# A state-space layer and an expert layer in one kernel: carried state folded into the products, first y products on ScalarE, expert weights split one step earlier

## The chip, the cores and the metric

The kernel runs on one core of one Trainium2 chip. Its metric is the device time of one execution in microseconds; the median of three runs before the change is 4197.73 us (4197.45 to 4197.76). Engines are named as in the profile: PE (TensorE), DVE (VectorE), ACT (ScalarE), POOL (GpSimd), SP (SyncE).

## The reference, cut to what matters

The input x is 8 images of 384 channels and 1024 tokens (32 x 32). Layer 0 adds to x a selective state-space block of the group-normed input; layer 1 adds a mixture of four experts of the group-normed result.

```
x = x + L0(group_norm(x))                 # 32 groups of 12 channels
  t  = layernorm(t);  xm, z = split(t @ in_proj.T)          # 384 -> 2 x 768
  xc = silu(causal_conv3(xm) + conv_b)                      # 3 taps along the tokens
  dt, B, C = split(xc @ x_proj.T)                           # 24, 16, 16
  dt = softplus(dt @ dt_proj.T + dt_b)
  h[l] = exp(dt[l] * A) * h[l-1] + (dt[l] * xc[l]) * B[l]   # 768 channels x 16 states
  y = sum_n h[l, :, n] * C[l, n] + D * xc;  y = y * silu(z)
  t = gelu(y @ out_proj.T @ w1.T + b1) @ w2.T + b2
x = x + L1(group_norm(x))
  scores = softmax(x @ gate_w + gate_b);  the two best experts weigh w
  out = sum_e coef_e * (relu(x @ w1_e + b1_e) @ w2_e + b2_e)
```

All of it is in float32. In layer 1 every operand is split into a high and a low part in fp32r, and three products of these take the place of one.

## The kernel before, in words

**Layer 0** works on 16 units, each half an image (512 tokens; the first half of an image has `half` 0, the second `half` 1). It runs as a software pipeline of 18 steps, n = -1 to 16: in step n unit n is scanned ("mid"), unit n + 1 is prepared ("pre": layer norm MU and VAR, projection and convolution XM, XP, C's transposition CT, dt DT), and unit n - 1 is finished ("post": y's transposition Y, output projection O, MLP M1 and M2). Step -1 is the prologue: it has no scan.

The scan of a unit has 32 slots k, 16 states in each of two groups of 384 channels; a slot has three scans of 128 channels x 512 tokens. In a slot POOL forms the product `vv` = (dt * xc) * B for all three (`scan_pool`, L575), two buffers deep; ACT forms exp(dt * A) into one of two PSUM banks (`scan_act`, L586); DVE scans them into `hh` (`scan_dve`, L615). PE transposes `hh` 128 tokens at a time (`scan_pe`, L675) into one of two banks `ht`, and DVE multiplies each of these four pieces by C and adds it to y (`mac_dve`, L661; for state 0 it is a plain product, L659). One of the four pieces in some states ("spread", by SPREAD_MASK) goes to ACT and POOL instead (L633, L645). A scan of a second half starts from the last column of the first half's scan, which ACT copied to `hl` (`last_act`, L593).

What lies between the scans is set by a written-out ORDER of stages for PE, with pads, and by LAGS, which say how many slots after PE's work the stage's ACT, DVE and POOL parts stand in their engines' own order. Each engine executes its instructions in that order. DVE takes up to DVE_QUOTA dense instructions after a scan. SP issues nearly all loads; POOL issues those of the gate and of the expert weights.

**The prologue.** DVE computes the group statistics of the first image (`group_stats`), then its own part of the preparation of unit 0; between them it computes `bn_stats` of the 14 other half images (`stat_dve`, L1172), all queued behind its first instruction of that step. The products over groups (L321) multiply by a 384 x 384 matrix `group`, nine blocks. At the end of the prologue the aggregates of the other images go through the same chain (`rest_dve`, `rest_act`, `rest_pe`), DVE, PE, DVE, PE, ACT, DVE, ahead of the first scan. For unit 0, POOL forms the layer norm's product with rstd (L920), the convolution's sums (L967) and the two products with dt (L1060, L1062).

**The last step** (n = 16) has no scan. PE runs O, M1, M2 of the last unit and, between them, the gate's logits of seven images, for which POOL loads x1 back (`gate_load`, L1218). After these loads POOL loads the raw expert weights w1, w2 (2.36 MB each, L1509) into `big`.

**Layer 1** begins with the gate of the last image: statistics (L233, L321 to L332, L340), logits (L275), top 2. Meanwhile ACT rounds the raw weights to `we_hi` (`split_act`, L1856) and POOL subtracts (`split_pool`, L1849) to `we_lo`, four of each at the start and four after. The first unit's products with w1 (`first_mm`) are spread in PE's order between the gate's. Then a loop over the units follows, bound by PE.

Of the kernel before, what the change touches and what calls it, by code (L numbers as in the profile page):

```python
# [13 lines left out]

# [11 lines left out]
P = 128  # L26
# [21 lines left out]
DVE_QUOTA = 1  # L48

# [4 lines left out]
ORDER = ("Y3 Y4 Y5 pad:3:0:3 DT3 pad:5:0:10 DT4 GN0 pad:5:19:6 O0 O1 DT5 O2 MU0 M1.0 pad:1:0:0 "  # L54
# [4 lines left out]
LAGS = {"Y.dve": 1, "Y.pool": 1, "Z.act": 0, "O.act": 0, "M1.act": 0, "M2.dve": 1, "MU.dve": 1,  # L59
        "MU.act": 2, "VAR.act": 0, "VAR.pool": 5, "XM.act": 0, "XM.pool": 2, "XM.act2": 2,  # L60
        "XP.act": 7, "XP.sync": 1, "CT.dve": 8, "DT.act": 1, "DT.pool": 5, "GN.act": 3,
# [14 lines left out]

DENSE_SLOTS = 31
SPREAD_LAG = 3
# [6 lines left out]
BURST_QUOTA = 3  # L85
SPREAD_MASK = 10818
# [6 lines left out]
MACS = [(k, c) for k in range(SLOTS) for c in range(CH) if not spread(k, c)]  # L93
# [42 lines left out]
def build(nc, a, out):  # L136

    with ExitStack() as ctx:
# [8 lines left out]
        w_d = nc.dram_tensor("top_weights", (KTOP, NB, L), F32).ap()  # L147

# [16 lines left out]
        layer0(nc, a, sem, psum, ident, st1, gn0, eps, x_d, x1_d, b_d, big, vv, consts, gate)  # L165
        layer1(nc, a, sem, psum, ident, eps, x1_d, w_d, out_d, consts, big, gate)
# [136 lines left out]

def group_stats(dve, act, pe, dv, ac, pc, mv, group, bank, tmp, gn, eps, tag, affine=False,
# [9 lines left out]
    if pe is not None:  # L314
        for src, dst, mark in ((mv[:, :, :, 0], mean_ps, "mean"), (tmp, var_ps, "var")):
# [3 lines left out]
            for m in range(KC):  # L319
                for k in range(KC):  # L320
                    mm = pe.matmul(dst[:, m, :], group[:, k, m * P:(m + 1) * P], src[:, k, :],  # L321
                                   start=(k == 0), stop=(k == KC - 1))
# [29 lines left out]
def layer0(nc, a, sem, psum, ident, st1, gn0, eps, x_d, x1_d, b_d, big, vv, consts, gate):  # L352
    with ExitStack() as ctx:
# [35 lines left out]
        hl = sb("hl", [P, NS, KD])  # L389
        yy = sb("yy", [P, CH, DI])  # L390
# [88 lines left out]
        e_da, e_v, e_scan = ev("dA", SLOTS * G3), ev("v", SLOTS), ev("scanned", SLOTS * G3)  # L479
        e_ht, e_mac, s_hl = ev("hT", SLOTS * CH), ev("mac", len(MACS)), sem("h_last")  # L480
        e_sc, e_ad = ev("scaled", len(SPREADS)), ev("added", len(ADDS))
# [51 lines left out]

        def bank_free(eng, units, name, i):


            pos = place[(name, i)]
            same = [s for q, s in enumerate(order[:pos]) if q % NDB == pos % NDB and s[0] in units]
# [30 lines left out]
        def scan_pool(eng, u, k):  # L569
            g, n = scan_of(k)  # L570
            if n == 0:
# [3 lines left out]
            e_v.inc_by(eng.tensor_tensor(  # L575
                vv[:, k % 2, :, :], wu[:, G3 * g:G3 * g + G3, :],
                bb[:, k % NBB:k % NBB + 1, :].to_broadcast([P, G3, T]), ALU.mult))
# [22 lines left out]
        def scan_dve(eng, u, k, i):  # L600
            g, n = scan_of(k)
            j = G3 * g + i
            if i == 0:
# [7 lines left out]
                elif k >= 2:  # L611
                    wait_last(eng, u, k - 2)
# [908 lines left out]
def layer1(nc, a, sem, psum, ident, eps, x1_d, w_d, out_d, consts, big, gate):  # L1521
    with ExitStack() as ctx:
# [345 lines left out]
        def first_mm(eng, q):  # L1868

            u, e, m = Unit(0, 0), q // KC, q % KC  # L1870
            if m == 0:
                eng.wait_ge(s_wlo, e + 1)
# [160 lines left out]
```

## Time and profile before

| | us |
|---|---|
| median of 3 runs | 4197.73 |
| the profiled execution, its own time | 4199.85 |
| its span, first to last instruction | 4198.2 |
| first scan | 93.44 |
| last step of layer 0 ends, layer 1 begins | about 3372 |
| PE, DVE, ACT, POOL busy | 3836.2, 3485.8, 2588.7, 2585.2 |

The times in the profile are microseconds from the span's start. "Busy" adds up recorded durations; where an engine starts an instruction before the record of the one before has ended, these overlap, so that time in a row is read from the starts. "Idle before" an instruction names the event that ended the idle time. PE's float32 matmul of 512 columns is two instructions in the trace.

### The profile page before, as it was taken

What the parts mean: (1) busy time and instruction counts of PE and PEld (TensorE: products, weight loads), DVE (VectorE), ACT (ScalarE), POOL (GpSimd) and SP (SyncE); (2) the same over time, 40 slices, a digit from 0 to 9 for tenths busy, and PEclk for the clock granted to TensorE, in tenths of its full rate; (3) what the DMA queues carried; (4) which work ended last, traced back from release to release, by engine and by line L of the source; (5) the groups of instructions that cost most, each with busy time, mean ns of one, the idle gap of its engine ahead of it and who ended that gap; (6) DMA issues with size and microseconds to landing.
All of it is one profiled execution on the core that took longest, in us unless ns stands there. A gap on an engine that the chain in (4) does not pass through costs nothing. (4 is left out here: it accounts for less than half of the span.)

```text
span 4198.2 us, 48613 instructions
## 1 busy us (share of the span) xinstructions
PE 3836.2 (91%) x15575; PEld 2300.2 (55%) x15575; DVE 3485.8 (83%) x4627; ACT 2588.7 (62%) x4102; POOL 2585.2 (62%) x1314
## 2 busy tenths in 40 slices
PE   6679898989998989989898989899979979999999
PEld 4344545455444544544544455445544468888887
DVE  5899999999999999999999999999999155555555
ACT  4667676767677776767676767676755233343433
POOL 3778787777878787878787878778876120000000
PEclk8779999999999999999999999999989989999999
DMA  5122222222222222222222222222222511111110
GB/s 179 43 70 66 89 67 85 73 83 78 84 68 88 69 89 88 70 92 66 88 66 89 67 85 80 82 72 88 64 83 74 202 56 53 40 40 40 40 40 36
DMA packets 147748, 317.90 MB, mean 76 GB/s; under 512 B 15388, under 2 KB 15772, under 8 KB 147012
## 3 DMA queue, kind: packets, MB, share of 16 engines
q1 hardware_dynamic: 139936, 281.74, 20.7%
q0 software_dynamic: 6832, 28.99, 1.9%
q10 hardware_dynamic: 756, 4.44, 0.3%
q8 instruction: 109, 1.79, 0.2%
q14 instruction: 115, 0.94, 0.1%
HBM read 289.36 MB, written 25.76 MB: 75 GB/s over the span
## 5 line engine op out<-in xcount | busy, mean ns | idle before, releaser
L575 POOL TENSOR_TENSOR vv<-big,bb 128x1536 f32<-128x1536 f32 x512 | 1767.4, 3453 | 595.1 <-DVE hh L615 579.8
L586 ACT ACTIVATE bank<-big,a_neg 128x512 f32<-128x512 f32 x1536 | 1045.3, 689 | 795.4 <-DVE hh L615 791.2
L675 PEld LDWEIGHTS bank<-ident,hh 128*128 128x128 f32 x6144 | 758.6, 146 | 1092.1 <-DVE yy L661 508.1
L675 PE MATMUL bank<-ident,hh 128*128 128x128 f32 x6144 | 1026.6, 289 | 258.0 <-DVE yy L661 161.9
L661 DVE SCALAR_TENSOR_TENSOR yy<-bank,ct,yy 128x384 f32<-128x384 f32 x1760 | 1036.1, 601 | 135.5 <-PE bank L675 131.8
L615 DVE TENSOR_TENSOR_SCAN hh<-bank,hl,vv 128x512 f32<-128x512 f32 x768 | 972.2, 1273 | 25.5 <-ACT bank L586 14.5
L615 DVE TENSOR_TENSOR_SCAN hh<-bank,vv 128x512 f32<-128x512 f32 x768 | 926.3, 1214 | 37.5 <-POOL vv L575 19.1
L795 PE MATMUL bank<-tt,wring 128*128 128x512 f32 x1152 | 556.4, 596 | 17.1 <-ACT tt L781 16.3
L826 PE MATMUL bank<-hid,wring 128*128 128x512 f32 x1152 | 553.0, 596 | 1.8 <-DVE xr L842 1.8
L1745 POOL DMA_DIRECT2D out<-xb x16 | 12.2, 765 | 777.3 <-DVE xb L1740 777.3
L1696 ACT ACTIVATE big<-bank,vv 128x512 f32<-128x512 f32 x180 | 123.9, 688 | 366.7 <-PE bank L1601 366.7
L932 PE MATMUL bank<-xn,w_in 128*128 128x512 f32 x576 | 285.0, 607 | 7.2 <-POOL xn L920 5.0
L747 PE MATMUL bank<-xn,w_in 128*128 128x512 f32 x576 | 283.6, 598 | 0.0
L771 PE MATMUL bank<-xc,w_out 128*128 128x512 f32 x576 | 278.5, 600 | 0.0
L1715 DVE TENSOR_TENSOR big<-big 128x512 f32<-128x512 f32 x188 | 126.9, 689 | 176.6 <-ACT big L1696 176.6
L795 PEld LDWEIGHTS bank<-tt,wring 128*128 128x128 f32 x1152 | 192.2, 191 | 135.0 <-issue 108.3
L826 PEld LDWEIGHTS bank<-hid,wring 128*128 128x128 f32 x1152 | 194.8, 192 | 124.1 <-issue 120.9
L967 POOL TENSOR_TENSOR xc<-xc,xm 128x510 f32<-128x510 f32 x192 | 226.1, 1179 | 23.0 <-ACT xc L957 15.4
L1599 PE MATMUL bank<-hb_hi,we_hi 128*128 128x512 f32 x576 | 225.7, 392 | 6.3 <-DVE hb_lo L1720 6.3
L1599 PE MATMUL bank<-xg_hi,we_hi 128*128 128x512 f32 x576 | 225.5, 391 | 0.0
L1600 PE MATMUL bank<-hb_lo,we_hi 128*128 128x512 f32 x576 | 225.4, 391 | 0.0
L1601 PE MATMUL bank<-hb_hi,we_lo 128*128 128x512 f32 x576 | 225.4, 391 | 0.0
(179 smaller groups left out, 5027.1 us busy)
## 6 DMA issues: line engine op xcount, KB each, us to landing
bb<-b_rows SPq DMA_DIRECT2D x512, 256.0 KB, 3.3
wring<-in_w_m SPq DMA_DIRECT2D x192, 384.0 KB, 3.1
xn<-in_x SPq DMA_DIRECT2D x16, 768.0 KB, 4.7
xr<-in_x SPq DMA_DIRECT2D x16, 768.0 KB, 6.1
x_scratch<-xr SPq DMA_DIRECT2D x16, 768.0 KB, 5.1
xb<-x_scratch SPq DMA_DIRECT2D x16, 768.0 KB, 4.5
out<-xb POOLq DMA_DIRECT2D x16, 768.0 KB, 4.0
big<-in_x SPq DMA_DIRECT2D x14, 768.0 KB, 5.5
```

Of the source, the lines that this page charges most:

```text
L575: e_v.inc_by(eng.tensor_tensor(vv[:, k % 2, :, :], wu[:, G3 * g:G3 * g + G3, :], bb[:, k % NBB:k % NBB + 1, :].to_broadcast([P, G3, T]), A ...
L586: e_da.inc_by(eng.activation(da[t % NDA][:, :], dt[:, j, :], ACT.Exp, scale=a_neg[:, j, n:n + 1]))
L615: e_scan.inc_by(eng.tensor_tensor_scan(hh[:, k % 2, i, :], da[(G3 * k + i) % NDA][:, :], vv[:, k % 2, i, :], start, ALU.mult, ALU.add))
L661: ins = eng.scalar_tensor_tensor(out=y, in0=ht[c % NHT][:, 0:G3 * P], scalar=scale, in1=y, op0=ALU.mult, op1=ALU.add)
L675: ins = eng.transpose(ht[c % NHT][:, i * P:(i + 1) * P], hh[:, k % 2, i, c * P:(c + 1) * P], ident[:, :])
L747: ins = eng.matmul(bank("Z", j)[:, :], w_in[:, k, DI + j * P:DI + (j + 1) * P], xn[:, w.half, k, :], start=(k == 0), stop=(k == KC - 1))
L771: ins = eng.matmul(bank("O", m)[:, :], w_out[:, k, m * P:(m + 1) * P], xc[:, u.half, k, :], start=(k == 0), stop=(k == KD - 1))
L795: ins = eng.matmul(bank("M1", m)[:, :], w[:, m % 2, k, :], tt[:, k, :], start=(k == 0), stop=(k == KC - 1))
L826: ins = eng.matmul(bank("M2", i)[:, :], w[:, k, :], hid[:, k, :], start=(k == 0), stop=(k == HH - 1))
L932: ins = eng.matmul(bank("XM", j)[:, :], w_in[:, k, j * P:(j + 1) * P], xn[:, v.half, k, :], start=(k == 0), stop=(k == KC - 1))
L967: ins = eng.tensor_tensor(y[:, d:T], y[:, d:T], xm[:, j % 2, tap, 0:T - d], ALU.add)
L1599: eng.matmul(bank, w[0], hi, start=start, stop=False)
```

## The change

- **Scan.** In second halves the scan starts from 0.0. The carried state times the decay of the first token is added to the first column of `vv` by POOL, one 128 x 3 add a slot (`scan_pool`), behind a wait on its own product. The decay is exp(A * dt[0]): POOL forms the product (`carried_log`), ACT the exponential (`carried_act`), POOL multiplies `hl` with it (`carried_state`), once for each group of 16 slots.
- **State 0.** The first product of each y piece goes from DVE to ACT (`init_act`), in the slot after, between the exponentials.
- **Prologue.** For unit 0, DVE does the product with rstd, the convolution (two multiply-adds a tile, from a single copy of the projection) and, for tiles 0 to 2, the two products with dt. Its silu is one batch of six. The statistics of the other half images lie between these. Their chain over groups moves into step 0, among MU and XM, with POOL and ACT doing parts of it. In all products over groups, blocks of `group` without a shared group are left out (7 of 9 remain).
- **Expert weights.** POOL loads them at the start of the last step, ahead of the gate's x1; in that step ACT rounds and POOL subtracts one expert part at a time, and POOL stores both parts in DRAM (`we_d`). Layer 1 loads them with SP, 16 loads of 0.59 MB between the loads of x1.
- ORDER, LAGS, SPREAD_MASK (five of sixteen states as before), SPREAD_LAG (3 to 5) and BURST_QUOTA (3 to 1) have new values.

```
-ORDER = ("Y3 Y4 Y5 pad:3:0:3 DT3 pad:5:0:10 DT4 GN0 pad:5:19:6 O0 O1 DT5 O2 MU0 M1.0 pad:1:0:0 "
...
+ORDER = ("Y3 Y4 Y5 pad:3:0:0 pad:5:0:12 DT3 GN0 pad:5:19:7 O0 DT4 DT5 O1 O2 MU0 M1.0 M1.1 "
...
-SPREAD_LAG = 3
+SPREAD_LAG = 5
-BURST_QUOTA = 3
-SPREAD_MASK = 10818
+BURST_QUOTA = 1
+SPREAD_MASK = 10310
...
+def shared_groups(m):
+    first, last = m * P // GN_CH * GN_CH, ((m + 1) * P - 1) // GN_CH * GN_CH + GN_CH - 1
+    return range(first // P, last // P + 1)
...
+            product = eng.tensor_tensor(
+                vv[:, k % 2, :, :], wu[:, js, :],
+                bb[:, k % NBB:k % NBB + 1, :].to_broadcast([P, G3, T]), ALU.mult)
+            if not u.half:
+                e_v.inc_by(product)
+                return
+            e_vp.inc_by(product)
+            if k == 0:
+                carried_state(eng, u, 0)
+            eng.wait_ge(s_h0, u.b * NG + g + 1)
+            eng.wait_ge(e_vp.sem, u.b * SLOTS + k + 1)
+            first = vv[:, k % 2, :, 0]
+            e_v.inc_by(eng.tensor_tensor(first, first, hl[:, n, js], ALU.add))
...
-            start = hl[:, n, j:j + 1] if u.half else 0.0
             e_scan.inc_by(eng.tensor_tensor_scan(
                 hh[:, k % 2, i, :], da[(G3 * k + i) % NDA][:, :], vv[:, k % 2, i, :],
-                start, ALU.mult, ALU.add))
+                0.0, ALU.mult, ALU.add))
...
+        def init_act(eng, u, k, c):
+            g, n = scan_of(k)
+            if c == 0:
                 e_cc.wait(eng, u)
                 e_yt.wait(eng, u, G3 * g + G3 - 1, back=1)
             e_ht.wait(eng, u, CH * k + c)
+            e_in.inc_by(eng.activation(y_part(g, c), ht[c % NHT][:, 0:G3 * P], ACT.Copy,
+                                       scale=ct[:, u.half, c, n:n + 1]))
...
+                def conv_dve(eng):
+                    e_xe.wait(eng, v, j)
+                    x, y, w = xm[:, j % 2, 0, :], xc[:, 0, j, :], conv_w[:, j, :]
+                    eng.tensor_scalar(halo[:, j, 0:2], x[:, T - 2:T], w[:, 0:1], None, ALU.mult)
+                    eng.tensor_scalar(halo[:, j, 2:3], x[:, T - 1:T], w[:, 1:2], None, ALU.mult)
+                    for tap in range(2):
+                        d = 2 - tap
+                        if tap:
+                            e_cv.wait(eng, v, 2 * j)
+                        e_cv.inc_by(eng.scalar_tensor_tensor(
+                            out=y[:, d:T], in0=x[:, 0:T - d], scalar=w[:, tap:tap + 1],
+                            in1=y[:, d:T], op0=ALU.mult, op1=ALU.add))
...
+                        if (k - 1) % NS == 0 and t >= G3 * k + NDA:
+                            for c in ((0, 1), (2,), (3,))[t - G3 * k - NDA]:
+                                init_act(eng, scan, k - 1, c)
...
+                for i, (tile, src) in enumerate(consts.weights):
+                    eng.dma_start(tile, src).then_inc(s_eraw[i], 16)
+                gate_load(eng, range(0, 4))
+                for q in range(2 * E):
+                    gate_load(eng, range(4 + q, 5 + q))
+                    expert_low(eng, q)
...
+            load_x1(eng, 0, 0)
+            load_weights(0)
             for h in range(HALVES):
                 eng.dma_start(last_x[h], x1_d[EARLY, :, :, h * T:(h + 1) * T]).then_inc(s_x[h], 16)
+            for q in range(1, E):
+                load_weights(q)
+            load_x1(eng, 0, 1)
+            for q in range(E, 2 * E):
+                load_weights(q)
             eng.wait_ge(*gate_marks()["twt"])
```

## Rows read from the trace of the kernel before

**Rows 1.** The page, busy time of the whole span.
```profile
PE 3836.2 (91%) x15575; PEld 2300.2 (55%) x15575; DVE 3485.8 (83%) x4627; ACT 2588.7 (62%) x4102; POOL 2585.2 (62%) x1314
```
**Rows 2.** Busy by window: length, PE, PEld, DVE, ACT, POOL, clock, DMA.
```profile
2470.33:2666.56 196.23, 181.89 (x718) 98.75 (x718) 183.47 (x234) 139.33 (x231) 159.07 (x86) 0.98 0.24 80
2666.56:2866.34 199.78, 183.24 (x718) 97.25 (x718) 188.56 (x235) 142.75 (x216) 157.95 (x74) 0.98 0.24 79
```
**Rows 3.** Groups by line and shape, whole span: busy, mean ns, idle before.
```profile
L615 DVE TENSOR_TENSOR_SCAN hh<-bank,hl,vv 128x512 f32<-128x512 f32 x768 | 972.2, 1273 | 25.5 <-ACT bank L586 14.5 <-POOL vv L575 10.7
L615 DVE TENSOR_TENSOR_SCAN hh<-bank,vv 128x512 f32<-128x512 f32 x768 | 926.3, 1214 | 37.5 <-POOL vv L575 19.1 <-ACT bank L586 14.8 <-issue 3.1
...
L633 ACT ACTIVATE ys<-bank,ct 128x384 f32<-128x384 f32 x128 | 74.3, 581 | 100.1 <-PE bank L675 100.1
L659 DVE TENSOR_SCALAR yy<-bank,ct 128x384 f32<-128x384 f32 x128 | 73.8, 597 | 0.0
```
**Rows 4.** Timeline of DVE in a first-half and a second-half scan: start, us.
```profile
97.91 0.59 DVE L659 TENSOR_SCALAR yy<-bank,ct 128x384 f32<-128x384 f32 x1
98.42 1.21 DVE L615 TENSOR_TENSOR_SCAN hh<-bank,vv 128x512 f32<-128x512 f32 x1
99.55 0.59 DVE L659 TENSOR_SCALAR yy<-bank,ct 128x384 f32<-128x384 f32 x1
...
3078.72 1.27 DVE L615 TENSOR_TENSOR_SCAN hh<-bank,hl,vv 128x512 f32<-128x512 f32 x1
3079.91 0.59 DVE L661 SCALAR_TENSOR_TENSOR yy<-bank,ct,yy 128x384 f32<-128x384 f32 x1
```
**Rows 5.** Waits of DVE in the second-half step 2666.56 to 2866.34: us, times, longest.
```profile
DVE yy L661 <- PE bank L675: 8.1, 17, 1.5
```
**Rows 6.** POOL's groups: in step 2666.56 to 2866.34, and over the span.
```profile
L575 POOL TENSOR_TENSOR vv<-big,bb 128x1536 f32<-128x1536 f32 x33 | 113.9, 3452 | 38.0 <-DVE hh L615 36.9 <-ACT ys L633 1.1
...
L970 POOL TENSOR_TENSOR xc<-xc,halo 128x2 f32<-128x2 f32 x48 | 9.4, 196 | 0.0
```
**Rows 7.** Timeline of the prologue, POOL, ACT and DVE.
```profile
39.44 3.74 POOL L920 TENSOR_TENSOR xn<-xn,rstd 128x512 f32<-128x512 f32 x3 [38.85 <-ACT rstd L915]
69.97 1.95 ACT L978 ACTIVATE xc<-xc,conv_b 128x512 f32<-128x512 f32 x3
...
86.67 6.81 POOL L575 TENSOR_TENSOR vv<-big,bb 128x1536 f32<-128x1536 f32 x2
...
90.07 3.45 DVE L335 SCALAR_TENSOR_TENSOR gn<-gn 128x21 f32<-128x21 f32 x1 [4.67 <-ACT gn L346]
93.44 4.55 DVE L615 TENSOR_TENSOR_SCAN hh<-bank,vv 128x512 f32<-128x512 f32 x4
```
**Rows 8.** Timeline at layer 1's start, after one prologue and one last-step row.
```profile
16.17 0.17 DVE L330 TENSOR_TENSOR xr<-xr 128x3 f32<-128x3 f32 x1
...
3295.70 0.28 ACT L1287 ACTIVATE vv<-bank 128x128 f32<-128x128 f32 x1 [7.02 <-PE bank L275]
...
3372.95 4.00 PE L321 MATMUL bank<-vv 128*128 128x1 f32 x18 [5.01 <-DVE vv L233]
...
3373.77 10.33 POOL L1849 TENSOR_TENSOR we_lo<-big,we_hi 128x1152 fp32r<-128x1152 f32 x4 [35.18 <-ACT we_hi L1856]
...
3379.02 2.53 DVE L330 TENSOR_TENSOR vv<-vv 128x3 f32<-128x3 f32 x1
...
3390.80 2.79 PE L275 MATMUL bank<-land,vv 128*32 128x128 f32 x48
```
**Rows 9.** Busy by window, columns as in rows 2, while the raw weights load.
```profile
3337.00:3347.00 10.00, 10.00 (x85) 4.81 (x87) 0.68 (x4) 4.75 (x7) 1.59 (x3) 1.00 0.94 356
```
**Rows 10.** Timeline of PE, matmuls and transposes in a row.
```profile
906.47 0.59 PE L771 MATMUL bank<-xc,w_out 128*128 128x512 f32 x1
906.90 0.49 PE L675 MATMUL bank<-ident,hh 128*128 128x128 f32 x3
907.23 1.88 PE L771 MATMUL bank<-xc,w_out 128*128 128x512 f32 x4
```

More of the change, by code:

```diff
@@ L48 @@
 DVE_QUOTA = 1
+PE_A = 4
+PE_B = 8
 ZB = 3
@@ L319, in group_stats @@
             for m in range(KC):
-                for k in range(KC):
+                near = shared_groups(m)
+                for k in near:
                     mm = pe.matmul(dst[:, m, :], group[:, k, m * P:(m + 1) * P], src[:, k, :],
-                                   start=(k == 0), stop=(k == KC - 1))
+                                   start=(k == near[0]), stop=(k == near[-1]))
             mm.then_inc(pc[0], 1)
@@ L532, in bank @@
             return dense[place[(name, i)] % NDB]
+        s_stat, s_rpe, s_ract = sem("stat_done"), sem("gn_rest_pe"), sem("gn_rest_act")
+        s_rpool = sem("gn_rest_pool")
+        in_first = [next(q for q, s in enumerate(order) if q % NDB == r and s[0] != "post")
+                    for r in range(NDB)]
+        rest_pos = max(in_first)
+        assert rest_pos > place[("MU", 0)]
+        rest_bank = dense[rest_pos % NDB]
+        rest_before = [s for q, s in enumerate(order)
+                       if q % NDB == rest_pos % NDB and s[0] == "pre"][-1][3]
         def bank_free(eng, units, name, i):
             pos = place[(name, i)]
+            if units["step"] == 0 and pos == rest_pos:
+                eng.wait_ge(s_ract, 1)
+                return
             same = [s for q, s in enumerate(order[:pos]) if q % NDB == pos % NDB and s[0] in units]
@@ L667, in scan_pe @@
             back, last = (0, (at // CH, at % CH)) if at >= 0 else (1, (SLOTS - 1, CH + at))
-            if spread(*last):
+            if last in INITS:
+                e_in.wait(eng, u, INITS.index(last), back=back)
+            elif spread(*last):
                 e_sc.wait(eng, u, SPREADS.index(last), back=back)
@@ L1208, in gate_marks, with gate_load @@
             return {k: (gv.sem, v) for k, v in gv.at.items()}
[L1210 to L1215 removed]
+        def gate_load(eng, loads):
+            if 0 in loads:
+                e_zp.wait(eng, Unit(NB - 1, 1))
+                e_op.wait(eng, Unit(NB - 1, 0))
+                e_st.wait(eng, Unit(EARLY - 1, 1))
+            for n in loads:
                 if n >= 4:
@@ L1348, in step @@
             bursts, act_slot = set(), 0
+            others = range(HALVES, NU)
+            stats = iter([lambda eng, m=m: stat_dve(eng, m) for m in others])
+            between = {"MU": [scale_dve, next(stats)], "VAR": [bias_dve, *islice(stats, 3)]}
             for entry in entries:
@@ L1443, in step @@
                             scan_act(eng, scan, t)
+                        if scan.half and t == NDA - 1:
+                            carried_act(eng, scan, 0)
                     if not scan.half:
@@ L1576, in layer1 @@
         glp, gtp = psum[4:6], psum[6:8]
-        s_wlo = sem("b3_split_low")
+        s_w = [sem(f"expert_w{q}") for q in range(2 * E)]
         def ev(name, per_unit, step=1):
@@ L1946, in _ @@
             def _(eng):
-                for h in range(HALVES):
-                    load_x1(eng, 0, h)
                 gate_sync(eng)
```

273 lines of the change are left out of this document (183 added, 90 removed), and 20 rows, old and new, of tables (LAGS, ORDER).

## The prediction

> **What bounds the kernel now.** First the page's busy line, to see that no engine is simply full [rows 1]. Then busy time by stage, with the windows cut where DVE copies C: sixteen scan steps of alternating length hold some 3160 of 4198 us, so their binding wait decides. A step whose scan has the second half of an image takes 199.8 us, one with a first half 196.2 [rows 2]. Then the groups by line: the scan has two forms, 1273 ns where it starts from the carried column `hl` and 1214 ns where it starts from 0.0 [rows 3]. The timeline of DVE shows what they cost in a row, since an instruction starts before its predecessor's end is recorded: from scan to next instruction 1.13 us without `hl`, 1.19 us with it, and 0.51 us for one update of y [rows 4]. In a second-half step DVE is busy 188.6 of 199.8 us, PE 183.2, POOL 158.0, ACT 142.8 [rows 2]. The waits say who waits for whom there: DVE waits for PE's transposes 8.1 us in 17 pieces [rows 5], while POOL stands idle 38.0 us ahead of its products, nearly all of it for scans of DVE [rows 6]. So DVE is the bound of the steady part with PE close behind it; ACT and POOL follow.
>
> **The steady part.** Two things leave DVE. First, eight `tensor_scalar` a step (the first product of each of four y parts in two groups, 128 in all [rows 3]) become activations: 8 x 0.51 = 4.1 us a step, 16 x 4.1 = 65 us of DVE time. Second, in the eight second-half steps all 96 scans start from 0.0: 96 x 0.06 = 5.7 us a step, 46 us together. DVE is relieved of 111 us.
>
> How much of that is time? The kernel before holds its own experiment. Its two kinds of step differ on DVE by just these 5.7 us of scan time, and in length by 199.78 - 196.23 = 3.55 us [rows 2]: 0.63 of it. The comparison isn't clean (a first-half step has 32 small copies of `hl` on ACT, and the halo instructions on ACT and POOL lie in different steps), so I hold 0.3 and 1.0 as bounds and take 0.63: 0.63 x 111 = 70 us.
>
> What the rest is lost to: in the slot after a group's first scan step DVE now has only three scans (3.4 us) and some dense work, while ACT has three exponentials (0.69 us each) and four of the new activations at 0.58 us, the price of the same shape in the spread parts [rows 3], 4.4 us in all. Behind each new activation on ACT's queue stands the next exponential, and behind that the scan; PE's next transposes now wait for ACT to free the bank. POOL's product of 3.46 us [rows 6] also outlasts three scans. So of the 2.04 us that a group gives, some 0.5 to 1 us comes back as waits, 16 to 32 us over 32 groups; that is inside the share of 0.63.
>
> What is added for the scans: in a second-half step POOL adds 3 columns to each product, 32 times, and waits for its own product before it. The nearest row is a 128x2 add of 196 ns [rows 6]; with two short gaps 0.3 us, so 10 us a step, to which come two products of 48 columns and two short logarithm products. Cover: POOL's 38 us of idle time. At 158 + 12 = 170 of some 193 us it still isn't the bound, and one late product (3.8 us against a slot of 5.5) is made good within a slot. Bounds of the addition: nothing, or the 1.3 us a slot from which it decides (below). The exponential of h0 at a step's start follows the last scan on ACT while DVE still has four y updates (2 us); I take nothing.
>
> The spread set keeps its size (five of sixteen), order, lags and PE's pads are set anew. No row prices that: it can move the 8.1 us of PE waits a step [rows 5] either way. I take nothing, with 16 x -2 to +1.5 us as bounds.
>
> **The prologue.** The first scan starts at 93.44 [rows 7]. Before it stands the statistics' last step, DVE at 90.07 for 3.45 us; its input from ACT was there, and POOL's second product ends just there [rows 7]. With that chain one step on, the scan waits for POOL's first product, 86.67 + 3.4 = 90.1: 3.3 us saved, the lower bound. Ahead of that: both products of the first statistics run 14 instead of 18 instructions at 4.0 us for 18 [rows 8], 1.8 us; the product with rstd leaves POOL (3.74 us [rows 7]) for DVE at about 0.63 us each, 1.8 us. The convolution is then bound by DVE: two multiply-adds, 1.5 us (0.75 each, as three-input instructions of 512 columns take), and three `bn_stats`, 1.9 us, for each of six tiles, after three more such sets. I put its end at about 64.5 us, with the one silu batch of six (0.65 us each) at 68.5 instead of 71.9 (69.97 + 1.95 [rows 7]): 3.4 us in all up to there, so DVE's stats give back some of what was saved. The last three products with dt leave POOL for DVE (the scan's product follows them at 86.67 [rows 7]): ACT's chain ends 3.4 us earlier, at 79.9, two DVE instructions 1.3 us, POOL's product 3.4 us: first scan at 84.7, 8.7 us earlier. Upper bound 12 us.
>
> **Layer 1.** The weights' split leaves its start. In the trace POOL subtracts from 3373.77 for 10.33 us, and a DVE instruction of 3 columns takes 2.53 us in that time [rows 8], against 0.17 us for the same in the prologue, at 16.17, where POOL is idle [rows 8]; the three in the chain took 1.80 + 2.53 + 2.53, so 6.4 us go. The two products over the groups lose 4 of 18 instructions, 4.00 us each [rows 8]: 1.8 us. A later DVE pair gives 1 us. What is late next: the loads. x1's first half (0.79 MB), one expert's parts (1.18) and the gate's two halves (1.57) are 3.5 MB; at the 356 GB/s of a full stretch [rows 9] 10 us and some 2 us to land, 3384.5, where the logits would be ready to start at 3390.80 - 8.2 = 3382.6 [rows 8]: 2 us back. I take 7 us. All 12.6 MB need 35 us, to 3408, about when the weights' store must go out on the same queue (SP); if it stands behind them it costs a few us. Bounds 0 to 10.
> The last step of layer 0 gets eight conversions on ACT and eight subtractions on POOL. PE is its path; ACT idles there. POOL's loads of raw weights, 4.7 MB or 13 us, now stand ahead of the gate's x1 loads, issued from 3270 on; the first logits' copy comes at 3295.70 [rows 8], so the first load, landing at about 3286, has cover. I take nothing; without the cover it would be 5 us.
>
> A rule of the Trainium skill bears on this ("SBUF — State Buffer", section "SBUF: two separate sides"): VectorE with two SBUF inputs and GpSimd share an exclusive lock, and the later one waits the whole instruction. By that rule, the trace agrees: 2.53 us for three columns. The same rule speaks against the new subtractions in the last step, which would hold up DVE's sums there. With the rule the three instructions fall to 0.5 us, without it they would stay at 6.9 and layer 1 would gain 1 us only, 6 us less in the sum.
>
> **Sum.** 70 + 8.7 + 7 = 86. The profiled execution took 4199.85 us (span 4198.2), so 4114; it stands 2.1 us above the median of the three runs, 4197.73: 4112.
>
> **The rivals.**
> A: the whole relief is time, because the retimed order gives PE's transposes their place. For: DVE is busy 94% of a step [rows 2]. Against: the pair shows 0.63. 111 + 16 = 127 less, 4071.
> B: PE and ACT take over at once; only 0.3 of the relief counts, and prologue and layer 1 give 15: 33 + 15 = 48, 4150. For: PE is busy 183.2 of 199.8 us [rows 2]. Against: that overlaps. In a row a 512-column instruction takes 906.90 - 906.47 = 0.43 us and three transposes 0.33 [rows 10]; the code issues 288 of the first and 434 of the second a step, 172 us.
> C, slower: POOL becomes the bound of the second-half steps through the added column sums, each behind a wait on its own product. POOL has 199.8 - 158 = 42 us spare, 1.3 us a slot. First-half steps (8 x 4.1 x 0.63 = 21) and the ends (16) still give 37 us, so it is slower than before from 158 + 32a = 199.8 + 37/8 on, a = 1.45 us. At 2.5 us, what a tiny DVE instruction took when locked out [rows 8], it is 238 us a step: 8 x 38 - 37 = 267 more, 4465. Against: the 196 ns row.
> D: neutral, because the new order wastes in each step the 5.4 us that it would have given (86 / 16), as PE waits beside the 8.1 us of today [rows 5]: 4190 to 4206. Nothing in the trace speaks for it but that these waits depend on the order.
>
> **How the numbers follow.** Forecast 0.62 (4112, own range 4092 to 4132), A 0.12, B 0.19, D 0.03, C 0.04. Below 0.2% (8 us) a measurement of this kernel can't be told from no change. Range 4074 to 4152: it takes in most of A and B. Faster 0.94, same 0.02, slower 0.04.
>
> **What would show it.** All scans at 1214 ns; steps of nearly one length, 193 to 194 us, in both kinds; ACT with 128 more activations of 0.58 us; POOL's idle time in second-half steps down to 15 to 25 us; the wait of scans for POOL still under 5 us a step; first scan near 85; the 3-column instructions of layer 1 at 0.17 us. Wrong: steps still over 196 us, scans waiting for POOL over 1 us each, or DVE idle ahead of scans for ACT in the slots after a group's first.

## The result, and the profile after

The changed kernel takes 4155.41 us (median of 4 runs, 4153.58 to 4156.68), the kernel before 4197.74 (4197.45 to 4203.49): ratio 0.9896, 95% interval 0.9878 to 0.9913. It is 42 us faster where 86 were forecast, and lies outside the range by 3 us. The profiled spans are 4198.2 and 4151.8, 46.4 apart (changes are taken before rounding):

| part, from profiled spans | before | after | change | forecast |
|---|---|---|---|---|
| start to first scan | 93.4 | 83.3 | -10.2 | -8.7 |
| first to last scan (the sixteen steps) | 3160.0 | 3115.9 | -44.1 | -70 |
| last scan to the aggregate that opens layer 1 | 119.1 | 134.8 | +15.7 | 0 |
| aggregate to the store of the top weights | 43.8 | 36.8 | -7.0 | -7 |
| rest | | | -0.8 | 0 |

The line for the sixteen steps holds three unlike parts. Step 0 has no unit to finish and step 15 none to prepare; between them lie fourteen full steps. Cut at DVE's copies of C again, with the version `b_order` (the kernel before with the new order, lags and masks alone) and `f_tail` (the kernel after without its new wait, both below) beside them, in us:

| | before | `b_order` | after | `f_tail` |
|---|---|---|---|---|
| first scan to the second copy of C (step 0) | 196.9 | 190.1 | 189.5 | 189.2 |
| steps 1 to 14 | 2771.9 | 2774.4 | 2745.7 | 2725.8 |
| last copy of C to last scan (step 15) | 191.3 | 187.4 | 180.7 | 178.4 |
| mean of the seven first-half steps among 1 to 14 | 196.19 | 196.23 | 194.46 | 194.22 |
| mean of the seven second-half steps | 199.79 | 200.11 | 197.79 | 195.19 |

The rows of steps 1 to 14, before and after, columns as in rows 2:
```profile
290.30:3062.20 2771.90, 2561.10 (x10052) 1376.54 (x10052) 2604.19 (x3264) 1973.80 (x3123) 2216.63 (x1106) 0.97 0.24 79
272.74:3018.47 2745.73, 2557.03 (x10052) 1382.79 (x10052) 2516.42 (x3151) 2031.96 (x3249) 2271.41 (x1359) 0.97 0.25 80
```
So of the 44.1 us only 26.2 were gained in the fourteen full steps, 7.4 in step 0 and 10.6 in step 15. The forecast had 193 to 194 us for both kinds of step; they came to 194.5 and 197.8, the second over the 196 that it had named as a sign of being wrong.

The page of after, busy time of the whole span (the counterpart of rows 1):
```profile
PE 3821.5 (92%) x15543; PEld 2298.5 (55%) x15543; DVE 3386.0 (82%) x4528; ACT 2644.3 (64%) x4226; POOL 2628.1 (63%) x1601
```
DVE has 99.8 us less, ACT and POOL have taken 56 and 43. One first-half and one second-half step, cut at the copies of C as in rows 2, same columns:
```profile
2431.09:2625.43 194.34, 181.45 (x718) 97.97 (x718) 179.64 (x227) 143.65 (x239) 160.12 (x87) 0.97 0.25 83
2625.43:2823.95 198.52, 185.34 (x718) 100.33 (x718) 179.89 (x226) 146.59 (x226) 164.21 (x108) 0.96 0.24 77
```
DVE is now equally busy in both kinds (183.5 and 188.6 before [rows 2]), but the second-half step is still 4.2 us longer than the first-half one, and has itself become only 1.3 us shorter (by the means of seven 3.3 longer and 2.0 shorter). The groups, against rows 3, show the relief itself as forecast (one form of scan, 1213 ns; the first products gone to ACT at 580 ns), and a releaser that was not there before, `vv` from L621, the add of the carried state:
```profile
L679 DVE TENSOR_TENSOR_SCAN hh<-bank,vv 128x512 f32<-128x512 f32 x1536 | 1851.4, 1213 | 144.5 <-ACT bank L651 90.3 <-POOL vv L621 27.1 <-PE bank L747 13.2
...
L721 DVE SCALAR_TENSOR_TENSOR yy<-bank,ct,yy 128x384 f32<-128x384 f32 x1760 | 1033.6, 600 | 111.5 <-PE bank L747 106.5 <-DVE yy L721 0.3
...
L732 ACT ACTIVATE yy<-bank,ct 128x384 f32<-128x384 f32 x128 | 71.3, 580 | 10.8 <-PE bank L747 10.8
```
DVE's waits in the second-half step (us, times, longest, as in rows 5):
```profile
DVE yy L721 <- PE bank L747: 6.7, 16, 0.9
DVE hh L679 <- ACT bank L651: 5.8, 10, 1.8
DVE hh L679 <- POOL vv L621: 3.3, 2, 2.4
DVE hh L679 <- PE bank L747: 1.8, 2, 1.4
```
The 2.4 us is the first scan of the step. Over all eight second-half steps these first scans wait 20.8 us, 2.3 to 3.1 each; in the kernel before they waited 11.5 us, nearly all of it for POOL's product. The timelines of ACT, POOL and DVE there show its chain:
```profile
2621.15 0.21 ACT L658 ACTIVATE hl<-hh 128x3 f32<-128x3 f32 x1 [2.59 <-DVE hh L679]
2621.38 1.28 ACT L829 ACT_TABLE_LOAD   x1
2622.67 1.85 ACT L829 ACTIVATE big<-bank,b_in 128x512 f32<-128x512 f32 x3
2624.54 1.28 ACT L753 ACT_TABLE_LOAD   x1
2625.83 1.30 ACT L651 ACTIVATE bank<-big,a_neg 128x512 f32<-128x512 f32 x2
2627.07 0.23 ACT L642 ACTIVATE h<-h 128x48 f32<-128x48 f32 x1
```
```profile
2621.56 3.45 POOL L609 TENSOR_TENSOR vv<-big,bb 128x1536 f32<-128x1536 f32 x1
2627.44 0.33 POOL L636 TENSOR_TENSOR hl<-hl,h 128x48 f32<-128x48 f32 x1 [2.43 <-ACT h L642]
2627.85 0.20 POOL L621 TENSOR_TENSOR vv<-vv,hl 128x3 f32<-128x3 f32 x1
```
```profile
2625.43 0.21 DVE L1116 COPY ct<-bank 128x64 f32<-128x64 f32 x1
2628.08 1.22 DVE L679 TENSOR_TENSOR_SCAN hh<-bank,vv 128x512 f32<-128x512 f32 x1 [2.44 <-POOL vv L621]
```
Read it backwards: the first scan of the second half waits for the add, the add for POOL's product with the factors, that for ACT's exponential of h0 (L642), and this stands behind the last copy to `hl`, which waits 2.59 us for the 96th scan, then a table load, three silus of z, a table load and two exponentials, 5.7 us in all.

In the last step of layer 0, five of ACT's eight roundings (L1493) wait for stores of earlier parts, 20.0 us together, and what stands behind them is late for PE. ACT, then PE:
```profile
3256.49 1.16 ACT L1493 ACTIVATE hh<-big 128x1152 fp32r<-128x1152 f32 x1 [4.83 <-DMA expert_parts<-hh]
...
3279.82 1.16 ACT L1493 ACTIVATE hh<-big 128x1152 fp32r<-128x1152 f32 x1 [6.67 <-DMA expert_parts<-hh]
3280.89 0.26 ACT L1441 ACTIVATE vv<-bank 128x128 f32<-128x128 f32 x1
```
```profile
3260.87 8.45 PE L898 MATMUL bank<-hid,wring 128*128 128x512 f32 x12 [5.87 <-ACT hid L882]
3281.21 0.47 PE L1427 MATMUL bank<-ident,vv 128*128 128x128 f32 x1 [5.64 <-ACT vv L1441]
```
DVE at the first scan, and at layer 1's three small products (2.53 us before for the one in rows 8):
```profile
83.29 2.34 DVE L679 TENSOR_TENSOR_SCAN hh<-bank,vv 128x512 f32<-128x512 f32 x2 [1.84 <-POOL vv L609]
...
3333.98 0.35 DVE L241 BATCH_NORM_AGGREGATE vv<-st 128x2 f32<-128x12 f32 x3 [3.16 <-PEq L1689]
...
3337.76 0.17 DVE L343 TENSOR_TENSOR vv<-vv 128x3 f32<-128x3 f32 x1
3337.97 0.17 DVE L345 TENSOR_TENSOR vv<-vv 128x3 f32<-128x3 f32 x1
3338.17 0.17 DVE L347 TENSOR_TENSOR vv<-vv 128x3 f32<-128x3 f32 x1
```

### The profile page after: what moved, and what is told of

Its sections match the earlier page's. It is cut to its first block and busy times, and to the rows that moved or that the text cites. A ratio compares the mean times of both kernels' runs of the same rounds, so it can differ in the third digit from the quotient of the medians.

```text
span 4151.8 us, 48913 instructions
## 1 busy us (share of the span) xinstructions
PE 3821.5 (92%) x15543; PEld 2298.5 (55%) x15543; DVE 3386.0 (82%) x4528; ACT 2644.3 (64%) x4226; POOL 2628.1 (63%) x1601
## 5 line engine op out<-in xcount | busy, mean ns | idle before, releaser
L679 DVE TENSOR_TENSOR_SCAN hh<-bank,vv 128x512 f32<-128x512 f32 x1536 | 1851.4, 1213 | 144.5 <-ACT bank L651 90.3
L747 PEld LDWEIGHTS bank<-ident,hh 128*128 128x128 f32 x6144 | 767.3, 147 | 1070.1 <-DVE yy L721 513.0
L747 PE MATMUL bank<-ident,hh 128*128 128x128 f32 x6144 | 1038.4, 291 | 243.3 <-DVE yy L721 151.6
L867 PEld LDWEIGHTS bank<-tt,wring 128*128 128x128 f32 x1152 | 192.0, 191 | 116.9 <-issue 114.1
L1808 PE MATMUL bank<-xg_hi,we_lo 128*128 128x512 f32 x576 | 224.8, 390 | 0.0
L1807 PE MATMUL bank<-xg_lo,we_hi 128*128 128x512 f32 x576 | 224.8, 390 | 0.0
```

The source lines that it names most:

```text
L679: e_scan.inc_by(eng.tensor_tensor_scan(hh[:, k % 2, i, :], da[(G3 * k + i) % NDA][:, :], vv[:, k % 2, i, :], 0.0, ALU.mult, ALU.add))
L747: ins = eng.transpose(ht[c % NHT][:, i * P:(i + 1) * P], hh[:, k % 2, i, c * P:(c + 1) * P], ident[:, :])
L867: ins = eng.matmul(bank("M1", m)[:, :], w[:, m % 2, k, :], tt[:, k, :], start=(k == 0), stop=(k == KC - 1))
L1807: eng.matmul(bank, w[0], lo, start=False, stop=False)
L1808: return eng.matmul(bank, w[1], hi, start=False, stop=stop)
```

## The experiments

"The kernel after" is 4155.41; below, a plain figure is the median, with the range of the runs behind it. In the cuts of code `...` stands for lines left out. "First-half" and "second-half" lengths are means of the seven steps of each kind among steps 1 to 14, unless a single window is named. Every version has one profiled run, and it need not be the median one: `f_tail`'s is the slowest of its five, `x_mac`'s too.

**One part undone, or one done alone.**

`u_carry`: the old start of the scans, and with it no factors and no add on POOL.
```
-                0.0, ALU.mult, ALU.add))
+                start, ALU.mult, ALU.add))      # start = hl[:, n, j:j + 1] if u.half else 0.0
```


> The kernel after, with the second halves' scans again starting from hl (no h0, no add on GpSimd). Theory W (each relief of VectorE is partly used up by a wait it creates): the 768 scans of the second halves cost 0.06 us more, 46 us in all, and against that the wait for the exponential of h0 at eight step boundaries (2.6 us each, 21 us) and the scans' waits for GpSimd (0.3 us a step more) go: 4155 + 46 - 21 - 5 = 4175, 4168 to 4182. The prediction's own rule (0.63 of what VectorE is relieved of): 4155 + 29 = 4184. Rival P (TensorE and its order pace the step, VectorE's work doesn't count): 4150 to 4158. If the 3.5 us by which a second-half step is longer stay as they are, they are not the scans' start.


4161.21 (4154.95 to 4164.66): only 6 us slower. A second-half step has 5.2 us more DVE work, its first scan waits 1.1 us for ACT instead of 2.6 for POOL, and it is 1.1 us longer. Theory W asked for 13 to 27 more and missed; the bound of rival P was passed by 3 us, and one run lies inside it.

`u_init`: the first products back on DVE.
```
-INITS = [(k, c) for k in range(0, SLOTS, NS) for c in range(CH)]
+INITS = []
...
```


> The kernel after, with the first y product of each group again on VectorE instead of ScalarE. Theory W: VectorE gets 8 x 0.51 = 4.1 us a step back (65 us in all), and its waits for ScalarE in the slots behind a group's first (about 2.5 of the 6 us a step) go: 4155 + 65 - 40 = 4180, 4172 to 4190. The prediction's rule: + 41, 4196. Rival P: 4150 to 4158. VectorE's waits for ScalarE at the scans fall from 6 us a step to 2 or 3 by W, stay by P.


4184.84 (4178.74 to 4186.10): worth 29 us, within W's range. A first-half step grows by 3.0 us, a second-half step by 1.0. Where I had also put the scans' waits for ACT down to the moved products, I was wrong: in a first-half step they fall only from 6.1 to 5.3 us. One thing here is not explained: a first-half step of `u_init` takes 197.5 us with DVE busy 183, one of `b_order` 196.2 with as much work on DVE, in the same order. The granted clock of steps 1 to 14 was 0.957 in `u_init` and 0.968 in `b_order` (0.969 in the kernel after), and no run parts the two. So in a first-half step it costs more to take the first products out (3.0 us) than they had brought against `b_order` (1.8).

`u_split`: the weights' split back at the start of layer 1 (loads, roundings and subtractions as before).


> The kernel after, with the split of the experts' weights back at the start of layer 1. Theory S (in layer 0's last step ScalarE's rounding waits 20 us for stores of the parts before, and the gate and its tail stand behind it): the last step loses 12 to 16 us, the start of layer 1 gains back 7: 4143 to 4150, last scan to aggregate 119 to 123 instead of 134.8. Rival O (the last step is longer because its work was reordered and TensorE's clock falls): the last step stays at 130 to 135, the time is 4160 to 4163.


4143.86 (4142.78 to 4144.39): 11.5 us faster than the kernel after. Last scan to aggregate is 117.2 instead of 134.8, and aggregate to weights' store 41.8 instead of 36.8. The move of the split cost 17.6 and gave 5.0. The two stalls of PE for ACT shown above, 5.87 and 5.64 us, and the slower matmuls behind them (the last section, 6.1 us) add up to the 17.6.

`b_order`: the kernel before with the new ORDER, LAGS and masks.


> The kernel before with the new order, lags and masks alone. Theory W (the order is fitted to the new load of the engines and brings nothing by itself): 4198 to 4215. Rival O2 (the order is a part of the gain that the prediction put down to VectorE's relief): 4170 to 4190; then the relief itself was worth less than 0.4 of its time. Rival P would have it near 4155 in the steps.


4193.07 (4190.58 to 4197.41, 11 runs), ratio 0.9987 (0.9978 to 0.9996): 5.5 us of the gain are the order's, between the two theories. All of it lies in steps 0 and 15 (6.8 and 3.9 us by the table above, from the fastest of its runs); steps 1 to 14 are 2.5 us longer together. DVE's waits for ACT at the scans are already 5.0 and 6.3 us in a first-half and a second-half step here: they came with the order.

**The wait at the step's start.** `f_h0`: the factors' logarithms at the end of the step before, their exponential ahead of the scans' first two.
```
-                    if scan.half and k == 0:
-                        carried_log(eng, scan, 0)
...
+                    if scan.half and k == 0:
+                        carried_act(eng, scan, 0)          # ACT, ahead of t = 0
...
-                        if scan.half and t == NDA - 1:
-                            carried_act(eng, scan, 0)
...
+                    if name == "pool" and k == end - 1 and pres and pres.half:
+                        carried_log(eng, pres, 0)
```


> The kernel after, with the first group's factors exp(A dt) of the next unit taken out of the step boundary: GpSimd computes their logarithms at the end of the step before, ScalarE's exponential stands ahead of the scans' first two. Theory W2 (the relief of the second halves' scans, 5.8 us a step, was eaten by this wait: with the scans started from hl a step pair took 1.0 us more, and VectorE waited 2.6 us less at the boundary): the 2.4 us wait for GpSimd and the 1.4 us for TensorE behind it go, 3 us x 8: 4155 - 24 = 4131, 4127 to 4140. Rival B2 (the second-half step has a bound of its own, TensorE and ScalarE, that takes the wait's place): 4150 to 4156, with the wait gone and others longer.


4140.81 (4135.58 to 4144.79): 14.6 us of the 24, just past the band. The eight first scans wait 11.9 us instead of 20.8. The rest of the wait stands, since the exponential is still behind the silus and their tables. ACT and DVE at one boundary:
```profile
2612.97 0.21 ACT L658 ACTIVATE hl<-hh 128x3 f32<-128x3 f32 x1 [2.59 <-DVE hh L679]
2613.19 1.28 ACT L829 ACT_TABLE_LOAD   x1
2614.48 1.84 ACT L829 ACTIVATE big<-bank,b_in 128x512 f32<-128x512 f32 x3
2616.35 1.28 ACT L753 ACT_TABLE_LOAD   x1
2617.64 0.24 ACT L642 ACTIVATE h<-h 128x48 f32<-128x48 f32 x1
```
```profile
2618.67 1.22 DVE L679 TENSOR_TENSOR_SCAN hh<-bank,vv 128x512 f32<-128x512 f32 x1 [1.92 <-POOL vv L621]
```
`f_h0_init`: the same with the first products on DVE.


> The same with the first y product of each group back on VectorE. W2: both reliefs are then worth about the same share everywhere, 8.2 us a step pair x 0.5 to 0.75: 4131 + 33 to 49 = 4164 to 4180, and a second-half step gains as much from ScalarE's products as a first-half one. B2: 4180 to 4185 as without the early factors, the gain of ScalarE's products in first-half steps alone.


4167.90 (4163.52 to 4172.66). It lies in W2's band, but only since `f_h0` itself came out 10 us above its own: the difference is 27 us, 0.42 of 65, below W2's share of 0.5. A second-half step gains half as much from ACT's products as a first-half one (1.2 and 2.3 us), where W2 had them equal.

`f_tail`: `f_h0`, and the last copy to `hl` in first-half steps behind the silus.
```
-                    if not scan.half:
+                    if not scan.half and k < SLOTS - 1:
                         last_act(eng, scan, k)
...
+                    if name == "act" and k == end - 1 and scan and not scan.half:
+                        last_act(eng, scan, SLOTS - 1)
```


> The kernel with the early factors of h0, and in first-half steps ScalarE's last copy to hl behind the silus of z (the trace of the early factors shows ScalarE idle 2.6 us for the 96th scan, then table load, three silus, table load, and only then the factors' exponential; GpSimd waits 1.2 and VectorE 1.9 us for it). Theory W2: with the silus in that gap the boundary into a second half waits 0.6 instead of 1.9 us or less, and 197.5 us steps become 195: 4140.8 - 10 to 18 = 4123 to 4131. Rival B2 (TensorE's transposes and clock take the wait's place): 4137 to 4142.


4128.37 (4127.87 to 4131.69): another 12.4, within W2's band. The silus use the 2.6 us in which ACT waited for the 96th scan, and six of the eight first scans wait for nothing; the other two wait 2.2 us together. ACT, DVE, and the second-half step's window:
```profile
2603.26 1.28 ACT L829 ACT_TABLE_LOAD   x1
2604.56 1.84 ACT L829 ACTIVATE big<-bank,b_in 128x512 f32<-128x512 f32 x3
2606.42 1.28 ACT L753 ACT_TABLE_LOAD   x1
2607.72 0.21 ACT L658 ACTIVATE hl<-hh 128x3 f32<-128x3 f32 x1
2607.83 0.23 ACT L642 ACTIVATE h<-h 128x48 f32<-128x48 f32 x1
```
```profile
2610.11 0.21 DVE L1116 COPY ct<-bank 128x64 f32<-128x64 f32 x1
2610.26 1.22 DVE L679 TENSOR_TENSOR_SCAN hh<-bank,vv 128x512 f32<-128x512 f32 x1
```
```profile
2610.10:2804.80 194.70, 181.65 (x718) 97.95 (x718) 179.63 (x226) 144.60 (x222) 163.69 (x107) 0.98 0.25 79
```
198.5 has become 194.7 (by the means 197.8 and 195.2), with DVE's work as it was. From `after` to `f_tail` it is 27 us by the medians and 22.4 by the profiled times from first to last scan; the waits of the eight first scans fell by 18.6. That the group of scans had waited 27.1 us for L621 in the kernel after is a chance likeness: 6.3 us of that stood elsewhere in the steps, and 8.5 us for L621 are left in `f_tail`. Two controls:

`u_carry_tail`: the old start of the scans with the late copy.


> The kernel after with the scans started from hl again and the last copy to hl behind the silus of z: against the kernel of early factors and late copy (4128.4) it differs in the new start of the scans alone. Theory W2 (the new start is worth the prediction's share once nothing waits for it: 0.5 to 0.63 of 46 us): 4151 to 4158, that is less than 6 below the 4161 that the old start gave without the late copy. Rival T (the late copy alone gave the 12 us, whatever the start of the scans): 4147 to 4151, and the new start is worth 20 or less.


4159.79 (4158.94 to 4161.71), 2 us above W2's band and far from rival T's. The late copy without the new start is worth 1.4 us by the medians (5.8 by the profiled times from first to last scan; `u_carry`'s runs spread over 10). So with next to nothing waiting for it, the new start is worth 4159.8 - 4128.4 = 31.4 us, 0.68 of its 46; with its wait it was worth 6. The profiled times from first to last scan give 3119.9 - 3093.5 = 26.4, or 0.57.

`b_tail`: the late copy in the kernel before.


> The kernel before with the last copy to hl behind the silus of z, alone. W2: VectorE's wait at the boundary there is for GpSimd's product (1.42 us), not for ScalarE, so nothing: 4195 to 4200. Rival T: 4186 to 4192.


4203.14 (4200.98 to 4209.59, 11 runs), ratio 1.0010 (1.0001 to 1.0019): no gain, if anything 4 us lost, beyond my 4200. Its first scans of second halves wait as before, 10.9 us.

`u_init_tail`: `f_tail` with the first products on DVE.


> The kernel of early factors and late copy (4128.4) with the first y product of each group back on VectorE, 65 us of its time. If the boundary waits were what kept this part below the prediction's 0.63: 4128 + 38 to 44 = 4166 to 4172. If the share of this part is smaller of itself (0.42 to 0.45 with the boundary waits in place, since each product stands ahead of an exponential on ScalarE and keeps a bank of TensorE): 4128 + 25 to 31 = 4153 to 4159.


4175.14 (4164.21 to 4178.91), above both bands: 47 us by the medians, 36 by the profiled spans (4165.5 and 4130.0), that is 0.55 to 0.72 of 65. This is what taking the first products out of the finished kernel costs; the runs spread over 15 us, too far to say more, and the doubt raised at `u_init` stands here too.

**Who bounds the step.** `x_mac` leaves out 376 of 384 columns in the 8 products a step of state 8 of each group.
```
-            y = y_part(g, c)
+            cols = 8 if n == 8 else G3 * P
+            y = yy[:, c, G3 * P * g:G3 * P * g + cols]
...
```


> The kernel after, in which the 8 products a step of state 8 of each group cover 8 of 384 columns: VectorE does about 8 x 0.45 = 3.6 us a step less, 58 us in 16 steps, every wait and signal stays. Theory E (VectorE and TensorE bound the step by turns, so a relief of either is worth about half: 49% for the first products between the kernel with and without them): 4155 - 20 to 35. The prediction's rule: - 36. Rival P (TensorE alone is the bound now): 4150 to 4157. Rival V (VectorE alone): - 50 or more.


4133.72 (4129.43 to 4146.71): -22 us, as theory E had it. DVE's busy time falls by 2.8 us a step, 45 us in all (the 58 of the expectation were too many), so the share is 0.5 by the median; over the five runs it lies between 0.2 and 0.6.

`x_pe` leaves out two of the three accumulated matmuls of each Z tile.
```
-                        ins = eng.matmul(..., start=(k == 0), stop=(k == KC - 1))
                         if k == KC - 1:
-                            e_zp.inc_by(ins)
+                            e_zp.inc_by(eng.matmul(..., start=True, stop=True))
```


> The kernel after without two of the three accumulated matmuls of each of the six Z tiles: TensorE does 12 x 0.45 = 5.4 us a step less, 86 us in 16 steps, VectorE's work unchanged. Theory E: 4155 - 25 to 50. Rival P: - 60 or more. Rival V: 4145 to 4157.


4137.52 (4130.88 to 4138.53): -18 us of 86, a share of 0.2, between theories E and V (PE's recorded busy time falls by 120 us, since the records of matmuls in a row overlap; by that the share is 0.15). By the medians a microsecond of DVE counts more than twice as much as one of PE, but `x_mac`'s runs spread too far to call the factor shown.

**The last step.** `f_split`: the rounding on POOL, which waits for the stores itself.
```
-                eng.activation(e_hi[q % 2].bitcast(F32R), e_raw[q], ACT.Copy).then_inc(s_ehi, 1)
+                eng.tensor_copy(e_hi[q % 2].bitcast(F32R), e_raw[q]).then_inc(s_ehi, 1)   # POOL
...
+                    expert_high(q)(eng)
                     expert_low(eng, q)
```


> The kernel after, with the rounding of the experts' weights in layer 0's last step on GpSimd (which waits for the stores itself) instead of ScalarE. Theory S (ScalarE's waits for the stores are what lengthens the last step): the last step loses 12 to 16 us and layer 1's start keeps its gain of 7: 4139 to 4143, below the 4143.9 with the split back in layer 1 by up to 5. Rival S2 (the stores and loads themselves, with 24 DMAs beside the gate's loads, lengthen it): 4150 to 4156.


4148.04 (4147.02 to 4150.80): 7 us faster than the kernel after, between the bands of S and S2. Last scan to aggregate is 128.5, so 6.3 of the 17.6 us are gone. ACT waits for no store, but now PE waits for the gate's loads (us, times, longest):
```profile
PE bank L283 <- DMA xn<-x_scratch: 4.9, 2, 4.0
PE bank L283 <- DMA xc<-x_scratch: 4.0, 2, 3.0
```
`f_split_late`: that split behind all of the gate's loads in POOL's queue.
```
-                gate_load(eng, range(0, 4))
+                gate_load(eng, range(EARLY * HALVES))
                 for q in range(2 * E):
-                    gate_load(eng, range(4 + q, 5 + q))
+                    expert_high(q)(eng)
                     expert_low(eng, q)
-                gate_load(eng, range(4 + 2 * E, EARLY * HALVES))
```


> The kernel after, with the experts' split on GpSimd alone and behind all of the gate's loads. Theory S3 (the loads that stand behind the split in GpSimd's queue are the other 11 us of the last step): the last step is 117 to 120 us as with the split in layer 1, and if the parts still land in time the start of layer 1 keeps its 7: 4136 to 4141. If they land late: 4142 to 4150, with the waits for the parts' tiles in layer 1. Rival S4 (the stores' traffic itself): the last step stays above 125.


4154.13 (4153.73 to 4155.80), above both bands of S3. The aggregate comes 133.5 after the last scan, past S4's 125 and nearly as late as in the kernel after, but PE waits for none of the gate's loads there:
```profile
3334.11 0.35 DVE L241 BATCH_NORM_AGGREGATE vv<-st 128x2 f32<-128x12 f32 x3 [19.46 <-PEq L1686]
```
DVE was done at 3334.1 - 19.5 = 3314.6, 114.1 after the last scan (by the same count 114.0 in `u_split` and 125.3 in `f_split`), and waits 19.5 us for the end of the block, which POOL holds up: its last store is issued at 3327.30. So with the loads ahead of the split the other 11 us are gone too (S3), but POOL's chain, 5.5 us a part, then ends last. A store of a high part lands 3.2 us after its issue here (median) and 8.4 in the kernel after, where loads share the queue. The Trainium skill ("DMA: Bandwidth & Descriptors", section "Anatomy of one DMA — SWDGE (gpsimd) path") gives 2.0 us and the bytes over 436 GB/s, for 0.59 MB an estimate of 3.4: the trace agrees for the first, not for the queue that is full.

`f_all_late`: both, split late and `f_tail`.


> The same on the kernel of early factors and late copy: by S3 with the parts in time 4109 to 4114, with them late 4116 to 4124, where 4120.8 is the version with the split in layer 1.


4131.71 (4129.69 to 4132.58), above both bands: POOL's late end costs as much as the split's other place does, here too.

`f_best2`: `f_tail` with the split in layer 1.


> The same with the experts' split back in layer 1, which took 11.5 us off the kernel after. If the two are independent: the kernel of early factors and late copy less 11.5, 4112 to 4120. Rival: 4125 or more, if the late copy brings nothing.


4120.76 (4118.40 to 4123.01), ratio to before 0.9811 (0.9798 to 0.9825), 1 us above the band. It beats both kernels, by 78 and 35 us; the two repairs add up but for 4 us.

## Why the prediction was wrong

- **The step that failed: the carried state's cost, taken at nothing.** "The exponential of h0 at a step's start follows the last scan on ACT while DVE still has four y updates (2 us); I take nothing." I looked at the four updates and not at ACT's queue between the last scan and the exponential: two table loads, three silus and two exponentials, 5.7 us against 2. Taking the wait away gives 27 us by the medians and 22.4 by the profiled times from first to last scan (`after` against `f_tail`; by `u_carry_tail` 1.4 to 5.8 of it may be the late copy by itself). That is most of the shortfall of the scan phase, 70 - 44 = 26. The Trainium skill ("ScalarE activation tables: per-element evaluation and per-set limits", section "What a function is on this engine") prices a change of function set at 1283 ns, and the trace agrees with 1.28 us. The profile of before had both loads at this place, on ACT:
```profile
2662.86 1.28 ACT L757 ACT_TABLE_LOAD   x1
...
2666.01 1.28 ACT L681 ACT_TABLE_LOAD   x1
```
- **The share of 0.63 was somewhat too high.** With the wait gone, taking either part out again costs 0.57 to 0.68 of its 46 us (the new start) and 0.55 to 0.72 of its 65 (the first products), which looks like 0.63. But these are the costs of undoing one part in an order that was fitted to both. From the other side, `f_tail`'s first-to-last-scan time is 66.5 us below before's, and 8.2 of that come with the order alone (`b_order`), which leaves 58.3 of 111 us, 0.53 (0.55 if the order is taken at its 5.5 us by the medians). In the fourteen full steps `f_tail` gained 46.1 of the 98 us of relief that the prediction counts there, 0.47; and the first-half steps, which have no new wait, got 1.73 us of their 4.1 in the kernel after, 0.42. The pair of steps of the kernel before gave an upper value; its second-half steps also held waits of 1.0 to 1.8 us at the first scan, so their 3.55 us need not be the scans' form alone.
- **The sum of the scan phase, term by term** (profiled times; it treats the terms as if they added up, which no run shows): 70 forecast, less 11.7 for the share, plus 8.2 for the order, less 22.4 for the wait, gives 44.1. The order was taken at nothing within -2 to +1.5 us a step, and in the fourteen full steps it was nothing; its gain in steps 0 and 15 was not foreseen, and it hid about a quarter of what the other two terms took.
- **The last step, "I take nothing": +17.6 us by `u_split`.** "PE is its path; ACT idles there" was true of ACT's time, not of its order. Five of the eight roundings wait for a store, and gelu and the gate's copies stand behind them. In the kernel after the two stalls of PE behind ACT, with the slower matmuls after them, make up all of the 17.6 us; once they are gone (`f_split`, 6.3 us) the gate's loads, which stand behind the split in POOL's queue, end last and keep 11.3. I had put this at up to 5 us, for the first load alone. The prediction also feared that POOL's new subtractions would hold up DVE's sums in the last step. The trace shows nothing of that: six DVE instructions started beside a subtraction of 2.63 us and took 0.17 to 0.24 us, but none of them reads two tiles in SBUF (L290 reads a PSUM bank and one tile, L278 one tile).
- **Layer 1's start: right in size.** 7.0 us; by `u_split` 5.0 are the split's; the other 2.0 fit the 1.8 forecast for the smaller products over groups, which no run has by themselves. The 3-column instructions take 0.17 us, as foreseen.
- **The prologue: right**, 10.2 for 8.7, with the first scan waiting for POOL's product, as worked out. With the order alone the first scan is already 1.5 us earlier (91.93 in `b_order`), though `b_tail`, where nothing of the prologue changed, had it at 91.52. No run takes the prologue's parts one by one.
- **The rivals.** A (4071) and D (4190 to 4206) are out by their times. B's time (4150) came closest, and its 0.3 is near what the full steps gave as built (26.2 of 98 us, 0.27), but not for its reason: without the wait they give 0.47 with the work of all engines as it was (`f_tail`), and relief of PE counts for little (`x_pe`). C is out: the add takes 0.20 us, and POOL is idle 26.7 us ahead of its products in a second-half step, at the edge of the 15 to 25 forecast.

What stays open: the runs of kernels with the first products on DVE spread over 7 to 15 us and have a lower granted clock, so their share isn't known better than above; why the new order gains in steps 0 and 15; why `b_tail` loses 4 us was not tried; and DVE's 6 us a step of waits for ACT, which the new order brought in exchange for waits for PE, was not taken apart. Nor was the relief tried without the new order. A version that splits in the last step and ends in time, with more buffers or the loads on another queue, was not tried either.

## What to carry to other kernels

When a change puts a new instruction into a chain between two engines, list what stands ahead of it in its own engine's queue at that moment, table loads included, and not only how idle the engine is: a 0.23 us exponential cost some 3 us a second-half step by its place. An engine with idle time is no free place for an instruction that waits for a DMA, since all behind it wait too. A share read from two kinds of step is at best the share of the work relieved; each new dependence at the boundary must be priced beside it. And a gain measured by undoing one part of the finished kernel can be larger than what the part gave when it was added, since the rest was fitted to it.

## What was not expected of the hardware

After a stall of 5.87 us in the last step, the next 12 instructions of PE took 8.45 us (3260.87, above), where 12 of the same line took 5.42 at 3270.15 with a granted clock of 1.00. In the 8.45 us it was 0.64, and 1.00 at 3250 to 3255, before the stall. The stretch around the other stall (5.64 us, 3281.21) had a granted clock of 0.66, so part of it at the lower of the two levels (1.2 GHz), part at the upper (2.4 GHz):
```profile
3260.87:3269.32 8.45, 8.45 (x13) 3.42 (x13) 0.00 (x0) 3.74 (x4) 5.40 (x6) 0.64 1.02 395
3280.00:3290.00 10.00, 8.79 (x36) 4.18 (x37) 0.34 (x2) 1.43 (x3) 4.52 (x4) 0.66 0.56 166
```
So a late operand cost PE its wait and some 3 us more: 3.03 after the first stall, and 3.04 after the second by the same count (0.47 us for the transpose instead of 0.27, 1.51 for the 24 gate matmuls instead of 0.86, and 7.61 for the next 12 instead of 5.42).
